# A transformer layer on one core: the last two heads by query half, and four orders of work changed

## What is computed

```python
q, k, v = x @ Wq[h], x @ Wk[h], x @ Wv[h]          # per head h, [1024, 64]
attn = softmax(where(causal, q @ k.T / 8, -inf))
y = x + concat_h(attn @ v) @ Wo
x1 = layernorm(x + gamma * norm(y, eps=1e-3) + beta)
h = silu(x1 @ wg.T) * (x1 @ wu.T)                  # integer weights over 127, hidden 768
out = layernorm(x1 + h @ wd.T)
```

## Time and profile before

| | |
|---|---|
| median of three runs | 1508.22 us |
| the profiled execution | 1508.49 us |
| its span in the profile | 1506.7 us |
| TensorE busy | 1413.7 us, 94% of the span |
| VectorE, ScalarE, GpSimd busy | 67%, 66%, 68% |
| chain that ended last, TensorE's share | 77% |
| mean granted clock of TensorE | 0.983 |

### The profile page before, as it was taken

One profiled execution on the slowest core, in us unless ns is written; L12 is line 12 of the kernel. 1 busy time (PEld: TensorE's weight loads), 2 busy tenths in 40 slices (PEclk: granted clock), 3 DMA queues, 4 the chain that ended last, 5 costly groups with the idle time before them and its releaser, 6 DMA issues.

```text
span 1506.7 us, 23750 instructions
## 1 busy us (share of the span) xinstructions
PE 1413.7 (94%) x7936; PEld 1226.0 (81%) x7936; DVE 1008.4 (67%) x2721; ACT 1001.6 (66%) x1921; POOL 1020.9 (68%) x966
## 2 busy tenths in 40 slices
PE   6999999999999999999999999999999999999646
PEld 5788888888888888888888888888888888888546
DVE  7666666666676666767676676776667676675346
ACT  4786767777776766767676676776667576676232
POOL 4676666666775867758676675867758586787664
PEclk9999999999999999999999999999999999999869
DMA  4223131313521221322132221221232112221000
GB/s 134 91 78 106 51 105 51 113 43 114 154 85 50 56 73 51 113 64 89 46 99 78 58 92 51 71 85 58 86 112 92 51 43 73 63 57 57 22 1 29
DMA packets 61482, 110.87 MB, mean 74 GB/s; under 512 B 16432, under 2 KB 41776, under 8 KB 61360
## 3 DMA queue, kind: packets, MB, share of 16 engines
q1 hardware_dynamic: 61360, 109.35, 24.3%
HBM read 61.34 MB, written 13.89 MB: 50 GB/s over the span
## 4 chain that ended last, share of the span: by engine, by line
PE 77%; DVE 10%; POOL 8%; ACT 3%; issue 2%; DMA 0%; ACTq 0%; SPq 0%; POOLq 0%; DVEq 0%
PE bank L659 21%; PE bank L637 15%; PE bank L538 12%; PE bank L612 8%; PE bank L599 8%; PE bank L563 5%; PE bank L705 5%; PE bank L717 3%; POOL h_lo L1154 2%; POOL probs_lo L1112 2%; DVE max_part L954 2%; POOL heads_T L1118 1%; DVE h_hi L1020 1%; DVE tanh_h L1021 1%; DVE tanh_h L1018 1%
## 5 line engine op out<-in xcount | busy, mean ns | idle before, releaser
L1112 POOL TENSOR_TENSOR probs_lo<-probs,probs_hi 128x512 fp32r<-128x512 f32 x576 | 743.4, 1298 | 414.0 <-ACT probs_hi L809 411.8
L806 ACT ACTIVATE probs<-bank 128x512 f32<-128x512 f32 x576 | 344.7, 598 | 302.5 <-DVE bank L968 238.9
L637 PE MATMUL bank<-Q,K 128*128 128x512 f32 (+3 forms) x1536 | 384.8, 352 | 4.7 <-ACT probs_hi L809 4.2
L809 ACT ACTIVATE probs_hi<-bank 128x512 fp32r<-128x512 f32 x576 | 342.8, 595 | 0.0
L637 PEld LDWEIGHTS bank<-Q,K 128*128 128x128 f32 x1536 | 252.9, 190 | 34.1 <-ACT probs_hi L809 5.8
L612 PE MATMUL bank<-K,Q 128*128 128x512 f32 (+3 forms) x768 | 247.0, 363 | 8.1 <-DVE max_part L952 5.8
L954 DVE TENSOR_REDUCE max_part<-bank 128x1 f32<-128x512 f32 x256 | 176.5, 690 | 103.9 <-PE bank L612 101.7
L952 DVE CUSTOM_DVE_ANT_0 bank<-bank,mask_keys_free 128x128 f32<-128x128 f32 (+3 forms) x512 | 243.7, 507 | 2.6 <-PE bank L612 2.3
L659 PE MATMUL bank<-probs_hi,VH 128*128 128x512 f32 (+3 forms) x768 | 231.5, 342 | 3.6 <-POOL probs_lo L1112 3.1
L659 PE MATMUL bank<-probs_hi,VL 128*128 128x512 f32 (+3 forms) x768 | 234.4, 346 | 0.0
L659 PE MATMUL bank<-probs_lo,VH 128*128 128x512 f32 (+3 forms) x768 | 234.3, 346 | 0.0
(11 more groups left out here) (135 smaller groups left out, 2252.4 us busy)
## 6 DMA issues: line engine op xcount, KB each, us to landing
Q<-Q SPq DMA_DIRECT2D x64, 256.0 KB, 3.6
K<-K SPq DMA_DIRECT2D x64, 256.0 KB, 3.4
recip_bc<-recip_scratch SPq DMA_DIRECT2D x64, 256.0 KB, 3.4
wh<-w_scratch SPq DMA_DIRECT2D x12, 768.0 KB, 4.4
wl<-w_scratch SPq DMA_DIRECT2D x12, 768.0 KB, 6.0
wo_quad<-wo SPq DMA_DIRECT2D x16, 256.0 KB, 3.4
y<-x SPq DMA_DIRECT2D x16, 256.0 KB, 3.9
x_tail<-x SPq DMA_DIRECT2D x13, 256.0 KB, 3.0
```

What stands on the lines that cost most here:

```text
L637: last = mm(bk[:, at:at + cols], KX[:, n, P * i:P * i + P], QX[:, n, q0:q0 + cols], start=(KX is K1 and at == 0), stop=(KX is K2 and at + ...
L806: A(pe_[:, g % 2, :], stb[g % 2][:, :], ACT.Exp).then_inc(exp_done, 1)
L809: A(ph[:, g % RING, :], stb[g % 2][:, :], ACT.Exp).then_inc(hi_done, 1)
L1112: G.tensor_tensor(pl[:, g % RING, :], pe_[:, g % 2, :], ph[:, g % RING, :].bitcast(F32), ALU.subtract).then_inc(lo_done, 1)
```

## The change

It has five parts.

1. The last two heads (`HA`, `HB`, numbers 62 and 63, both in one pair of heads_T) give up their nine steps each for one list of 18 steps (`LAST_STEPS`). Queries 0 to 511 of both heads are finished first (five steps); short pieces of both share steps. Each head has one of the banks `pvb`, for one query half at a time. For this, the banks of maxima of both heads and their transposes move ahead (`EARLY_MAX`, `EARLY_T`, steps 5 to 17 of iteration 15).
2. The four tails of the end are no longer in lock step. Each (`FINAL`, functions `f_...`) has steps of its own: the first two Wo units in steps 28 and 30 of iteration 15, the other two in steps 38 and 39. They have separate banks for down, so the three rounds accumulate in one bank and are added once; beta is added, and gamma and the scale applied, on VectorE in two fused operations; h_hi is now a copy on ScalarE. The extra tail (`LAST_B`) moves from steps 6 to 43 to steps 8 to 36.
3. Sums of the last two heads: queries 0 to 511 are copied with their 64 rows of sums and divided on VectorE (`last_norm_c0`: reciprocal of 256 columns, then a product, in steps 25 and 26); the second half of head 62 goes through the DMAs as before, that of head 63 is divided out of the bank (`last_norm_c1`, step 38). GpSimd's divisions of the pair before move to steps 26 and 27.
4. In TensorE's step `t_down` comes behind projections, Wo and V. Wo units 0 and 1 move from steps 11 and 13 to 12 and 14, the first down products from 12 to 13.
5. On VectorE the first operation of the GLU comes ahead of the bank of maxima, the two others stay where they were.

The diff, cut to its core:

```diff
+HA, HB = QH - 2, QH - 1
+LAST_STEPS = [
+    [(HA, 0, 0, 512)], [(HA, 1, 128, 384), (HA, 3, 384, 128)],
+    [(HB, 0, 0, 512)], [(HA, 2, 256, 256), (HB, 2, 256, 256)], [(HB, 1, 128, 384), (HB, 3, 384, 128)],
+    [(HA, 0, 512, 512)], [(HA, 1, 512, 512)], [(HA, 3, 512, 512)], [(HA, 2, 512, 512)], [(HA, 4, 512, 512)],
+    [(HA, 5, 640, 384), (HA, 7, 896, 128)],
+    [(HB, 0, 512, 512)], [(HA, 6, 768, 256), (HB, 6, 768, 256)],
+    [(HB, 1, 512, 512)], [(HB, 3, 512, 512)], [(HB, 2, 512, 512)], [(HB, 4, 512, 512)],
+    [(HB, 5, 640, 384), (HB, 7, 896, 128)],
+]
+LAST_AT = NG - len(LAST_STEPS)
+LAST_DONE = {(HA, 0): (3, 2), (HB, 0): (4, 3), (HA, 1): (12, 6), (HB, 1): (17, 7)}
 V_TILES = [(0, 1), (3, 6), (2, 4), (5, 7)]
...
+def pieces(g):
+    if g >= LAST_AT:
+        return LAST_STEPS[g - LAST_AT]
+    h, k = divmod(g, NS)
+    return [(h % QH, i, q0, cols) for i, q0, cols in PIECES[k]]
...
+EARLY_MAX = {5: [(0, 0)], 6: [(0, 1)], 7: [(0, 2), (0, 3)], 8: [(0, 4)], 9: [(0, 5), (0, 6)], 10: [(0, 7)], 11: [(0, 8), (1, 0)],
+             12: [(1, 1)], 13: [(1, 2), (1, 3)], 14: [(1, 4), (1, 5)], 15: [(1, 6), (1, 7)], 16: [(1, 8)]}
+EARLY_T = [12, 17]
...
-WO_AT, WO_AT_LAST, WO_AT_END = [11, 13, 15, 21], [11, 13, 15, 16], [9, 10, 11, 12]
+WO_AT, WO_AT_LAST = [12, 14, 15, 21], [11, 13, 15, 16]
...
-STEADY = tail_at(-5, -1, 7, [9, 23, 29], [12, 26, 32], 36)
-LAST_A = tail_at(-5, -1, 7, [9, 18, 22], [12, 21, 25], 29)
-LAST_B = tail_at(6, 10, 26, [28, 32, 36], [31, 35, 39], 43)
+STEADY = tail_at(-5, -1, 7, [9, 23, 29], [13, 26, 32], 36)
+LAST_A = dict(tail_at(-5, -1, 7, [9, 18, 22], [12, 21, 25], 30), LN3=27, LN3R=28, OUT=29)
+LAST_B = tail_at(8, 11, 19, [21, 25, 29], [24, 28, 32], 36)
...
+def final_at(xb, wo, tr, up, down):
+    return dict(XB=xb, WO=wo, YA=wo + 1, C1=wo + 1, R1=wo + 2, A1=wo + 2, R2=wo + 4, N2=wo + 4, TR=tr, X1=tr + 1,
+                UP=up, GLU=[a + 1 for a in up], HL=[a + 1 for a in up], DOWN=down, Y2=down[2] + 1, R3=down[2] + 2, N3=down[2] + 3)
+FINAL_LOAD_AT = [10, 17, 18, 19]
+FINAL = [final_at(17, 28, 33, [36, 38, 40], [38, 40, 42]), final_at(19, 30, 35, [37, 39, 41], [39, 41, 43]),
+         final_at(20, 38, 42, [44, 46, 48], [46, 48, 50]), final_at(21, 39, 43, [45, 47, 49], [47, 49, 51])]
...
+        f_xt = [two(raw[:, 1, :]), two(HT[:, 2, 0:CH]), two(HT[:, 2, CH:S]), x_tail[:, :, :]]
+        f_th = [th[:, :, :], two(raw[:, 0, :]), two(pe_[:, 0, :]), two(pe_[:, 1, :])]
+        f_bk = [(misc[0], misc[1], stb[0]), (mxb[0], mxb[1], stb[1]), (pvb[0], pvb[1], stb[0]), (misc[0], misc[1], stb[1])]
+        F = [Final(y[:, 2 * j:2 * j + 2, :], f_xt[j], *carved(X[:, 0:2, :], 4), f_th[j], *f_bk[j])
+             for j, X in enumerate((Q1, Q2, K1, K2))]
...
-            return misc[(u + 1) % 2] if wi == NIT - 1 else misc[(1, 1, 0, 1)[u]]
+            return (misc[1], misc[0], pvb[0], pvb[1])[u] if wi == NIT - 1 else misc[(1, 1, 0, 1)[u]]
...
+                    if u == 0:
+                        pe.wait_ge(tdve[0], ND * (XTRA - 1) + DV["y22"])
+                    elif u == 2:
+                        pe.wait_ge(ht_copied, copies_before(NH - 2, 1) + 1)
+                    pe.wait_ge(last_norm, u + 1)
...
+                        if g >= LAST_AT:
+                            bk, ends = pvb[n - HA], (g - LAST_AT, i) == LAST_DONE[n, c]
+                        else:
+                            bk, ends = pvb[c], (k + 1, i) in ((C0_DONE, 2), (C1_DONE, 7))
+                        last = mm(bk[:, b0:b0 + cols], VX[:, i, n // 2, v0:v0 + P], px[:, g % RING, at:at + cols],
+                                  start=(t == 0 and i == 0), stop=(t == 2 and ends))
...
-                    if ts in at["DOWN"]:
-                        t_down(n, at["DOWN"].index(ts), gset)
...
                     if v_due(g, u) is not None:
                         v_unit(v_due(g, u), u)
+                for n, gset, ts, at in tails(g):
+                    if ts in at["DOWN"]:
+                        t_down(n, at["DOWN"].index(ts), gset)
+                for j, r in finals(g, "UP"):
+                    f_up(j, r)
+                for j, r in finals(g, "DOWN"):
+                    f_down(j, r)
+                for j, _ in finals(g, "WO"):
+                    wo_unit(NIT - 1, j)
+                for j, _ in finals(g, "TR"):
+                    f_transpose(j)
...
+            def last_copy(h, c):
+                n, slot, cols = h % QH, (NH // 2 - 1) % 3, slice(CH * c, CH * c + CH)
+                own, other = (slice(0, E), slice(E, P)) if n == HA else (slice(E, P), slice(0, E))
+                act.wait_ge(pv_mm, acc_done(h, c) + 1)
+                if (n, c) == (HA, 0):
+                    act.wait_ge(wo_mm, 4 * (NIT - 1))
+                    act.wait_ge(sums_loaded, 16 * (NH - 2))
+                if c:
+                    A(HT[0:E + 1, slot, cols], pvb[n - HA][0:E + 1, :], ACT.Copy).then_inc(ht_copied, 1)
+                else:
+                    A(HT[own, slot, cols], pvb[n - HA][own, :], ACT.Copy)
+                    A(rsum[own, cols], pvb[n - HA][other, :], ACT.Copy).then_inc(ht_copied, 1)
...
+            def f_tanh(j, r):
+                act.wait_ge(fpe[j], FPE[f"g{r}"])
+                if r:
+                    act.wait_ge(fpool[j], FPL[f"hl{r - 1}"])
+                A(F[j].th, two(F[j].gate[:, :]), ACT.Tanh, scale=0.5 * WSCALE).then_inc(fact[j], 1)
+                act.wait_ge(fdve[j], FDV[f"h{r}"])
+                if r:
+                    act.wait_ge(fpe[j], FPE[f"d{r - 1}"])
+                A(F[j].hh, F[j].th, ACT.Copy).then_inc(fact[j], 1)
...
                 dve.wait_ge(tact[g], NA * n + AC[f"tanh{r}"])
-                V.scalar_tensor_tensor(T[g].th[:, :, :], T[g].th[:, :, :], 1.0, two(T[g].bk[0][:, :]), ALU.add, ALU.mult).then_inc(tdve[g], 1)
+                V.scalar_tensor_tensor(T[g].th, T[g].th, 1.0, two(T[g].bk[0][:, :]), ALU.add, ALU.mult).then_inc(tdve[g], 1)
+            def t_glu_up(n, r, g):
...
+            def f_ya(j):
+                y_add(NIT - 1, j)
+                dve.wait_ge(y_added, 4 * (NIT - 1) + j + 1)
+                f_stats(j, 1)
+            def f_c1(j):
+                f_own(j, "mv1b")
+                for t in range(2):
+                    V.scalar_tensor_tensor(F[j].rows[:, t, :], F[j].rows[:, t, :], f_stat(j).mv[:, t, 0:1], gm[:, :],
+                                           ALU.subtract, ALU.mult).then_inc(fdve[j], 1)
+            def f_a1(j):
+                dve.wait_ge(fpool[j], FPL["r1"])
+                f_own(j, "c1b")
+                for t in range(2):
+                    V.scalar_tensor_tensor(F[j].rows[:, t, :], F[j].rows[:, t, :], f_stat(j).rs[:, t:t + 1], F[j].xt[:, t, :],
+                                           ALU.mult, ALU.add).then_inc(fdve[j], 1)
+                f_own(j, "a1b")
+                f_stats(j, 2)
+            def f_x1lo(j):
+                dve.wait_ge(fact[j], FAC["x1hi"])
...
+            def last_norm_c0(q):
+                slot, cols = (NH // 2 - 1) % 3, slice(2 * P * q, 2 * P * q + 2 * P)
+                dve.wait_ge(ht_copied, copies_before(NH - 1, 0) + 1)
+                V.reciprocal(rsum[:, cols], rsum[:, cols]).then_inc(last_recip, 1)
+                dve.wait_ge(last_recip, 1 + q)
+                V.tensor_tensor(HT[:, slot, cols], HT[:, slot, cols], rsum[:, cols], ALU.mult).then_inc(last_norm, 1)
+            def last_norm_c1(q):
+                slot = (NH // 2 - 1) % 3
+                here, cols = slice(2 * P * q, 2 * P * q + 2 * P), slice(CH + 2 * P * q, CH + 2 * P * q + 2 * P)
+                if q == 0:
+                    dve.wait_ge(recip_bc, 16 * (NH - 1))
+                    V.tensor_tensor(HT[0:E, slot, CH:S], HT[0:E, slot, CH:S], rsum[0:E, CH:S], ALU.mult)
+                    dve.wait_ge(pv_mm, acc_done(NH - 1, 1) + 1)
+                V.reciprocal(rsum[E:P, cols], pvb[HB - HA][0:E, here]).then_inc(last_recip, 1)
+                dve.wait_ge(last_recip, 3 + q)
+                V.tensor_tensor(HT[E:P, slot, cols], pvb[HB - HA][E:P, here], rsum[E:P, cols], ALU.mult).then_inc(last_norm, 1)
...
-                if 0 <= g < NG and g % NS in DIAG:
+                if 0 <= g < NG and diagonal(g):
                     scores_mask(g)
-                h, rest = divmod(g + T_LEAD, NS)
-                if rest == 0 and 0 <= h < NH:
-                    max_row8(h)
-                h, k = divmod(g + MAX_LEAD, NS)
-                if 0 <= h < NH:
+                if transpose_due(g) is not None:
+                    max_row8(transpose_due(g))
+                for n, gset, ts, at in tails(g):
+                    if ts in at["GLU"]:
+                        t_glu(n, at["GLU"].index(ts), gset)
+                for h, k in max_due(g):
...
-                if k == 0 and 0 <= h < NH:
+                if k == 0 and 0 <= h < NH - 2:
                     recip(h)
+                if g == NG - 1:
+                    last_chain_recip()
+                if g == acc_done(NH - 1, 1) + LAG + 1:
+                    last_norm_c1(0)
...
```

(5 more changed lines are left out.)

468 lines of the change are left out of this document (291 added, 177 removed).

## The result

The kernel after takes 1461.61 us, the median of four runs from 1459.86 to 1462.55; the kernel before took 1508.53 beside it. The ratio is 0.9687 with a 95% interval of 0.9669 to 0.9706. Forecast were 1455 and a range of 1441 to 1471. The profiled execution has a span of 1459.7 us against 1506.7, so 47.0 us are gone, where 53.6 were forecast: inside the range, and 6.6 us short.

The account below looks back on a forecast made before the run. TensorE was taken to bound the body (busy 94%), but not the end. Gains of 13.5 (V unit), 5.0 (Wo) and 36.6 (end) less 1.5 (maxima) made 53.6 us: 1508.2 to 1454.6, say 1455, range 1441 to 1471.

Parts of the forecast that it names:

- V unit first: Step 32, iterations 5 to 14: V unit ahead of down products covers their 1.35 us wait for h_lo, gain 13.5 us.
- Wo one step on: Steps 12 to 14: Wo unit 0 no longer waits 0.50 us for the up bank, gain 5.0 us, bounds 0 and 6.
- GLU first: VectorE's GLU operation ahead of the bank of maxima: only order changes, gain 0, the 0.7 us wait in step 26 stays.
- Early maxima: Maxima of the last two heads in steps 5 to 16: a loss of 1.5 us, bounds 0 and 4.
- The end: From step 17 of iteration 15 to the end: 143.4 us becomes 106.8, so 36.6 us go.
- the full one: Steps 36 to 54: VectorE is the full engine, with about 20 us against TensorE's 17 in steps 38 to 43.
- The reciprocal: Four VectorE reciprocals of 256 columns, 1.5 us each; the two in step 38 cost 2 us.
- the four waits: TensorE's waits at step 28's down products, step 33's transposes, step 35's values and the second unit's transposes: sum 8.6 us.
- GpSimd and VectorE hold the end: Rival for the end: each wait repeats, twice the waits, 15 us more, 1470 us; chance 0.18.
- TensorE's pace: Rival for the end: order leaves slack, the stretch takes 92 to 97 us, total 1443; chance 0.17.
- The rest: Rivals: no steady gain, 1468 us, chance 0.07; slower, 1521, 0.02; change not doing as said, 1481, 0.03.
- The signs: Wrong if a new wait appears in steps 12 to 15 or 33, or final steps show VectorE idle while TensorE waits.

Follow-up runs that it names:

- the useless products: Kernel after with the extra tail's store two steps later, Wo units back in iterations without a tail, and unused matmuls where TensorE stands at the end: 1456.54 us.
- the store: Kernel after with only the extra tail's store moved from step 36 to 38 on the DMA queue: 1455.9 us.

## Why the prediction was right, point by point

- *V unit first*, 13.5: 13.9, shown alone by its run. The narrow margin of probs_lo held.
- *Wo one step on*, 5.0: 7.7 in the ten iterations, of which 2.4 were lost again in iterations 1 to 4. The 5.3 left are near the forecast, by two errors that cancel. "Iteration 15 keeps its old steps, so it is 10 x 0.50" left out the four iterations whose Wo units move too, and that a unit that moves takes its cover with it.
- *GLU first*, 0: 3.7 alone, 1.7 with the others, from a wait in step 26 that shrank by 0.17 us each time. "The wait in step 26 therefore stays" failed to that extent.
- *Early maxima*, a loss of 1.5: 1.0, or 1.3 against the kernel with the three steady edits and the old end, whose same steps take 43.3 us.
- *The end*, 36.6: 25.9, or 27.1 against the same kernel's end of 144.6. The mis-sized term. Its 106.8 us divide into 44.9 up to the last scores (issue 41.9 less 1.65 of step 35, and waits of 1.8 and 2.9) and 61.9 behind. Measured are 50.5 and 67.0.
  - Up to the last scores, +5.6. The wait of step 28 was 1.5 for 1.8, with another of 0.3 for h_lo beside it. The transposes of step 33 waited 4.3 for 2.9, two waits of 0.7 together were not foreseen, and the clock took about 1.4 (what the useless products gave back). Some 2 us are left that no view names.
  - Behind them, +5.1. By the views, TensorE's own time is 49.1 us for 41.8 of issue, some 10 us of it at 1.2 GHz; its waits are 10.9 for 12.7, and the time behind the last product is 7.0 for 7.5. As causes the runs show 2.3 for the store: "copied out in step 33, 9.3 us later is step 38 ... so it is hidden" counted the chain's own length and not the queue that it goes through. Two reciprocals at 1.75 in place of 1.5 make 0.5. The clock makes 0.4 behind the third unit's transposes, by the run that held it up there. Less the 0.5 behind the last product, some 2.4 us stay open.
  - The places of the waits were wrong as well. The last down products waited 1.38 for 2.4, the second unit's transposes 1.2 for 3.2. The transposes of the other two units, 4.3 forecast, waited 0.7; the first unit's last down products ahead of them in step 42 waited 4.5. And VectorE was "the full one" only from 1410 to 1420 (9.60 of 10 us); behind 1430 it is busy 12.1 of 21.5.
- *The reciprocal*, 1.5 by the row of 16 columns: 1.75. The Trainium skill's figure (VectorE: DVE Perf Modes, First, the fixed hardware budget) made it 2.1 as an estimate; the measurement lies between, and nearer to the row.
- *Slips in the working*, all small: the four waits 1.8, 2.9, 0.8 and 3.2 make 8.7, not 8.6; two reciprocals at 3.8 would have cost 6.6, not 6; the slices with a lower clock before are the third and second from the end, and none at the start.
- *The rivals.* The rival "GpSimd and VectorE hold the end" (1470) named the mechanism that shows, with 10.7 us of its 15. "TensorE's pace" was wrong in kind: the sum of 82 was passed by 35 us, not by 10 to 15. The rest didn't come.
- *The signs*. Two of those named for being wrong did show: a new wait of 1.16 us in step 12 of the iterations without a tail, and VectorE standing 2.80 us in step 38 ahead of a Wo unit that TensorE waits 1.32 us for. The last scores came 11.9 us later than before, not 3 to 8. A steady iteration takes 87.3 us, not 87.7 to 87.9.

The total lies in the range partly by luck. Steady and early parts brought 19.8 us for the 17.0 forecast, by a gain in the GLU that had been put at nothing and more from the Wo units, and that made up for a part of the 10.7 by which the end fell short. The steady mechanisms held; the end had its size wrong. The chief lesson is that the three engines' queues met where I had let them pass each other.

## What to carry to other kernels

A transfer that must be early is only as early as the first waiting transfer ahead of it in its queue: list the queue in order, with what each waits for, before calling a chain hidden. When a unit of work is moved away from a wait, look in every kind of iteration for what stands in its old place uncovered. And if TensorE waits for a chain of other engines, its clock and its order don't matter up to that wait: shorten the chain. They matter again in the block that the next chain starts from.
